# A five-stage hybrid transformer kernel: prologue order and buffers, paired block products in the delta attention, and the mixture's norm and stores moved into its body

## The chip, the cores and the metric

The kernel runs on one core of one Trainium2 chip. The metric is the device time of one execution in microseconds. The engines are TensorE (PE), VectorE (DVE), ScalarE (ACT), GpSimd (POOL) and SyncE (SP), which issues nearly all DMAs. All data are float32, and a float32 matmul shows in the trace as two matmul instructions (a transpose as one).

## What is computed

x has 4 sequences of 1024 tokens with 128 features. Four residual layers follow each other, each on a layer-normed x:

```python
x = x + delta_attention(layernorm(x))   # 8 heads; q, k, v by short convs (4 taps) and silu; beta, decay g
x = x + mixture(layernorm(x))           # 15 experts, top 3 of a softmax, and one shared expert
x = x + decay_attention(layernorm(x))   # 2 heads of 64, state decays by 1 - w
x = x + mixture(layernorm(x))
# delta attention, per token, head and each of 3 inner steps:
S = S * exp(g); S = S + b_i * k_i (v_i - k_i S); o = q S
# then o is rms-normed, gated with silu(x Wg) and projected by Wo
```

## The kernel before

**Prologue** (`prologue`, L124). Tokens lie as rows in four blocks. For each block TensorE turns the raw rows (`raw`) and the normed rows (`hat`) into feature columns, ScalarE keeps them (`keep_x` L248, `keep_xn` L259) and squares the centred rows (`square` L253), VectorE centres and norms, GpSimd takes the power -1/2. Then come the gates, a softplus chain on VectorE, and per head a table of decays: VectorE builds `gm` (L369, two buffers), TensorE sums it (L243), ScalarE exponentiates (L284), VectorE masks (L377), and SP stores it in four DMAs, 32 in all (L191). The loop's loads of the table wait for these stores.

**Delta attention** (`delta_attention`, L382) is a hand-scheduled software pipeline of 128 steps (8 heads by 16 spans of 64 tokens of all 4 sequences; U = 8 units of 32 tokens). A step runs through three stages in one loop over f: stage f projects, convolves and multiplies keys and queries into Gram products; stage c = f - 11 does values, gate and the inversion's block products; stage r = f - 12 runs the recurrence, in two halves cc. Every engine has its own written order (SP L640, GpSimd L731, ScalarE L865, VectorE L1020, TensorE L1238) and waits for the others through semaphores. An engine executes in order, so a wait holds up all behind it. The names that matter:

- `k_tile`, `v_tile`, `gate_tile` (L1122): projections into two PSUM banks PP; `tap0` (ScalarE L788) and `tap1` to `tap3` (VectorE L953) are the conv; `vsilu`, `ksilu`, `qsilu`, `gate_` the silu on ScalarE.
- `ktr`, `vtr` (L1173, L1195): transposes into TG; `ksum_`, `kr` read TG on ScalarE, `vr` (L993) on VectorE; `gram` (L1185), then `ap` (L982) on VectorE; `ss_`, `rinv_`, `step_`, `es_` small scales on VectorE, `rk_` on GpSimd.
- The results go through DRAM: `kqg_store`, `rec_store`, `ap_store` write, `rec_load`, `da_load`, `y_load`, `dec_load` read. Every fourth step (a group) `at_load` brings a 32-wide triangular system, `subst` solves it on GpSimd in 12 spots per step, `x_store` stores X, and `xt` (ScalarE L863) turns it.
- `zm` (L1204), `wm` (L1213), `m3` (L1221) join the inverted blocks: per unit a 64x64 product of `apkB` and `Dd` into the single bank ZW, then `zev` (L844, L845), `w12`, `yev` on ScalarE.
- The recurrence, per half: `ks` (L1076), `rhs_` (DVE L901), `w_` (L1086), `wev` (ACT L778), `sr` (L1096), `sup` (DVE L912, needs `sg` of GpSimd), and `o_` (L1111, L1112), `mo_`, `fo_`, `osb_`, `ot`, `og_`, `out`, `acc_` for the output.

```python
for u in range(U):                                   # zm, L1203
    last = mm(ZW[0:64, u, :], apkB[N % 2][:, u, :], Dd[N % 2][:, u, :], start=True, stop=True)
```

**Mixture** (`normed_mixture`, L1269, run as f1 and f2). First all 8 tiles of 512 tokens are normed in column layout: `centre` and `variance` by matmuls, square root on ScalarE, reciprocal on VectorE, `replicate`, `norm`. Router logits go over `r_lt` (L1364), `r_tr` (L1370), `r_sub` (L1491), `r_exp`, `r_top`, `r_ct` (L1376), `r_cwt` (L1524); SP stores the weights and loads them broadcast over the partitions (gates). Then for each tile and each of 16 experts: `hidden` (L1387), relu (L1470), scaling by the gate (L1558), second product (L1418). The router of tile n + 1 is placed in the body of tile n.

**Decay attention** (`decay_attention`) norms its tiles in row layout (L1663, L1873 to L1890, L1672); its near products (L1720) are 64x64 blocks on all four quarters of the array, the two row halves into two PSUM banks. **Store** (`store_rows`, L84): turns x back, four 512 KB DMAs on SP. Between stages stands a barrier of all engines.

## Time and profile before

| | us |
|---|---|
| median of 3 runs (lowest, highest) | 3255.2 (3253.8, 3260.7) |
| the profiled execution: time | 3252.4 |
| its span, first to last instruction | 3250.6 |
| prologue | 0 to 80 |
| delta attention | 80 to 2475 |
| mixture f1 | 2477 to 2764 |
| decay attention | 2765 to 2953 |
| mixture f2 | 2955 to 3239 |
| store | 3240 to 3250.6 |

PE is busy 94% of the span, DVE 78%, ACT 70%, GpSimd 60%. A row of a timeline has the start, the duration, the engine, the line of the kernel, output and inputs, the number of instructions merged, and in brackets the idle time before it with what ended it. A matmul's end is modelled and its duration overlaps the next one, so the distance of two starts tells what it held of the queue.

### The profile page before, as it was taken

The numbers are of one execution on the slowest core, as the hardware profiler recorded it, in microseconds if no ns is written. First come the engines' busy times: TensorE is split into PE (matmuls) and PEld (weight loads), VectorE is DVE, ScalarE is ACT, GpSimd is POOL, SyncE is SP. The second block draws the span as 40 slices with busy tenths as digits, with TensorE's granted clock in tenths as the row PEclk, the third lists the DMA queues.
The fourth block names the chain that finished last, engine by engine and source line by source line (L and its number), as shares of the span: only waits on it lengthen the run. The fifth ranks groups of instructions, "written<-read, shape, count | busy, mean of one in ns | idle before, by whom it ended". The sixth has DMA issues, their size and how long they took to land. (4 is left out here: it accounts for less than half of the span.)

```text
span 3250.6 us, 83664 instructions
## 1 busy us (share of the span) xinstructions
PE 3046.8 (94%) x27404; PEld 2373.9 (73%) x27404; DVE 2528.6 (78%) x5801; ACT 2265.4 (70%) x6879; POOL 1956.2 (60%) x3107
## 2 busy tenths in 40 slices
PE   5669999999999999999999999999998999768998
PEld 3458888888888888888888888888775444455444
DVE  5669999999999999999999999999654444684443
ACT  4678888888888888888888888888543333323333
POOL 1588888888888888888888888888720000100000
PEclk8779999999999999999999999999998999869999
DMA  4356776767677676767767677766532232002323
GB/s 100 113 153 172 186 183 174 181 173 182 168 190 179 176 181 169 182 174 188 182 170 183 171 175 178 190 180 165 141 95 83 107 145 98 10 2 76 147 98 124
DMA packets 587912, 482.88 MB, mean 149 GB/s; under 512 B 464492, under 2 KB 504076, under 8 KB 581340
## 3 DMA queue, kind: packets, MB, share of 16 engines
q1 hardware_dynamic: 587484, 477.53, 55.5%
q8 instruction: 225, 3.69, 0.5%
q14 instruction: 203, 1.66, 0.2%
HBM read 285.52 MB, written 191.86 MB: 147 GB/s over the span
## 5 line engine op out<-in xcount | busy, mean ns | idle before, releaser
L953 DVE SCALAR_TENSOR_TENSOR conv_k<-PP,tk,conv_k 128x256 f32<-128x256 f32 x1536 | 723.4, 479 | 62.9 <-ACT conv_k L788 35.1
L726 POOL TENSOR_TENSOR X<-X,tmp 96x31 f32<-96x31 f32 (+15 forms) x992 | 534.1, 538 | 77.7
L953 DVE SCALAR_TENSOR_TENSOR conv_v<-PP,tv,conv_v 128x256 f32<-128x256 f32 x1152 | 539.4, 477 | 45.1 <-ACT conv_v L788 35.5
L723 POOL TENSOR_TENSOR tmp<-At,X 96x31 f32<-96x31 f32 (+15 forms) x992 | 486.1, 490 | 63.0 <-DMA At<-n_d 4.8
L1122 PE MATMUL PP<-xn,wk 128*128 128x268 f32 x1024 | 344.6, 421 | 33.7 <-DVE conv_k L953 25.1
L709 POOL TENSOR_TENSOR rk<-ss,half 96x8 f32<-96x8 f32 x128 | 209.5, 1637 | 175.3 <-DVE ss L921 175.3
L691 POOL TENSOR_TENSOR Sg<-S,gend 128x512 f32<-128x512 f32 x256 | 266.1, 1039 | 59.3 <-DVE S L912 59.3
L760 ACT ACTIVATE recA<-TG,es 96x128 f32<-96x128 f32 x1024 | 284.9, 368 | 8.7 <-DVE es L946 8.7
L788 ACT ACTIVATE conv_k<-PP,tk 128x256 f32<-128x256 f32 x512 | 245.1, 480 | 60.1 <-PE PP L1122 53.4
L752 ACT ACTIVATE recA<-TG 128x128 f32<-128x128 f32 x1024 | 265.5, 272 | 25.3 <-PE TG L1173 25.3
L1086 PE MATMUL RB<-rhs,Yf 96*96 96x128 f32 x2048 | 269.1, 274 | 14.6 <-DVE rhs L901 14.3
L778 ACT ACTIVATE ws<-RB 96x512 f32<-96x512 f32 x256 | 151.6, 592 | 183.0 <-PE RB L1086 180.2
L1076 PE MATMUL RA<-S,kqgB 128*96 128x128 f32 x2048 | 276.2, 278 | 1.0 <-DVE S L912 1.0
L1096 PE MATMUL RA<-ws,recB 96*128 96x128 f32 x2048 | 271.1, 275 | 0.2 <-ACT ws L778 0.2
L1086 PEld LDWEIGHTS RB<-rhs,Yf 96*96 96x96 f32 x2048 | 242.2, 163 | 37.0 <-DVE rhs L901 24.6
L1096 PEld LDWEIGHTS RA<-ws,recB 96*128 96x128 f32 x2048 | 259.2, 192 | 8.0 <-ACT ws L778 0.8
L1185 PE MATMUL TG<-kq 128*96 128x128 f32 x1888 | 245.3, 273 | 1.2 <-ACT recA L760 1.0
L1076 PEld LDWEIGHTS RA<-S,kqgB 128*96 128x96 f32 x2048 | 233.4, 163 | 13.0 <-DVE S L912 4.4
L676 POOL TENSOR_TENSOR kqgA<-kq,gdec 128x768 f32<-128x768 f32 x128 | 203.2, 1588 | 39.3 <-ACT kq L829 32.6
L1122 PE MATMUL PP<-xn,wv 128*128 128x268 f32 x768 | 218.5, 391 | 2.3 <-DVE conv_k L953 2.3
L1185 PEld LDWEIGHTS TG<-kq 128*96 128x96 f32 x1888 | 219.0, 163 | 2.2 <-ACT recA L760 2.2
L1122 PEld LDWEIGHTS PP<-xn,wk 128*128 128x128 f32 x1024 | 163.8, 200 | 64.5 <-issue 34.5
(280 smaller groups left out, 6787.9 us busy)
## 6 DMA issues: line engine op xcount, KB each, us to landing
kqg_d<-kqgA SPq DMA_DIRECT2D x128, 512.0 KB, 6.2
kqgB<-kqg_d SPq DMA_DIRECT2D x128, 512.0 KB, 4.3
rec_d<-recA SPq DMA_DIRECT2D x128, 480.0 KB, 3.4
recB<-rec_d SPq DMA_DIRECT2D x128, 480.0 KB, 5.8
f1gates<-f1gates_d SPq DMA_DIRECT2D x24, 1024.0 KB, 6.7
f2gates<-f2gates_d SPq DMA_DIRECT2D x24, 1024.0 KB, 6.7
gdec<-gdec_d SPq DMA_DIRECT2D x128, 128.0 KB, 5.6
apk_d<-apkA SPq DMA_DIRECT2D x128, 128.0 KB, 3.3
```

What stands on the lines that cost most here:

```text
L691: nc.gpsimd.tensor_tensor(Sg[:, :, :], S[cc][:, :, :], d.broadcast_to([128, B, 128]), ALU.mult).then_inc(sg_ev[cc], 1)
L723: nc.gpsimd.tensor_tensor(t, At[q % 2][:, j, j + 1:].unsqueeze(2).broadcast_to(sh), X[q % 2][:, j, 0:cols].unsqueeze(1).broadcast_to(sh), ...
L726: nc.gpsimd.tensor_tensor(x, x, t, ALU.subtract).then_inc(sub_ev, 1)
L752: last = nc.scalar.activation(recA[N % 2][:, u * 128:(u + 1) * 128], TG[:, u, :], ACT.Square, accum_out=ksum[:, u:u + 1])
L760: last = nc.scalar.activation(recA[N % 2][0:R, u * 128:(u + 1) * 128], TG[0:R, u, :], ACT.Copy, scale=es[:, u, TC - 1:TC])
L788: nc.scalar.activation(acc, src[:, :, 0:SPAN], ACT.Copy, scale=w).then_inc(tap0_ev[i], 1)
L953: return nc.vector.scalar_tensor_tensor(acc, src[:, :, j:j + SPAN], w[:, j:j + 1], acc, ALU.mult, ALU.add)
L1076: last = mm(RA[0:R, b, :], kqgB[N % 2][:, b * NCC + cc, 0:R], S[cc][:, b, :], start=True, stop=True)
L1086: last = mm(RB[0:R, b, :], Yf[N % 2][:, b * NCC + cc, :], rhs[:, b, :], start=True, stop=True)
L1096: last = mm(RA[:, b, :], recB[N % 2][:, u * 128:(u + 1) * 128], ws[cc][:, b, :], start=True, stop=True)
L1122: mm(out, w, x, start=True, stop=True).then_inc(tile_mm[i], 1)
L1185: last = mm(gram_bank(N, hf)[0:R, u % HU, :], kq[N % 2][:, u, 0:R], kq[N % 2][:, u, :], start=True, stop=True)
```

## The change

The prologue's four engine orders change, `gm` gets four buffers, and the last of the four table stores of each head is issued by ScalarE. In the delta attention `apkB` and `Dd` hold their two halves of units on two partition halves, `zm` alternates between them, and their loads are split; `zev` reads the two halves; and all five written orders change. The mixture norms a tile in row layout inside the body, two tiles ahead, with three PSUM banks for `hidden` in place of four; logits come directly in row layout, with the bias added on VectorE (`r_sub`). In f2 each tile is turned back and stored by ScalarE one tile later, and the call of `store_rows` goes.

```diff
--- before.py
+++ after.py
...
-        gm = sb("gm", [128, 2, NC, TC])
+        DEEP = 4
+        gm = sb("gm", [128, DEEP, NC, TC])
...
+        def keep_table(eng, h, b):
+            eng.dma_start(g.edec_d[h, :, :, b, :], ex[TC * b:TC * (b + 1), h, :].rearrange("t (s x) -> t s x", x=SPAN)).then_inc(g.edec_out[h], 16)
...
             for h in range(NH):
                 sp.wait_ge(mask_ev, h + 1)
-                for b in range(B):
-                    sp.dma_start(g.edec_d[h, :, :, b, :], ex[TC * b:TC * (b + 1), h, :].rearrange("t (s x) -> t s x", x=SPAN)).then_inc(g.edec_out[h], 16)
+                for b in range(B - 1):
+                    keep_table(sp, h, b)
...
             raw(0)
             raw(1)
+            raw(2)
             hat(0)
-            raw(2)
+            raw(3)
             pe.wait_ge(w_in, 16 * 7)
             hat(1)
             gates(0)
-            raw(3)
             hat(2)
             gates(1)
+            gates(2)
             hat(3)
-            gates(2)
             gates(3)
...
+                square(q)
                 keep_x(q)
-                square(q)
-                if q:
-                    keep_xn(q - 1)
+                if q >= 2:
+                    keep_xn(q - 2)
+            keep_xn(B - 2)
             keep_xn(B - 1)
...
             for h in range(NH):
                 act.wait_ge(ge_mm, h + 1)
                 nc.scalar.activation(ex[:, h, :], GE[h % 2][:, :, :].rearrange("p a x -> p (a x)"), ACT.Exp).then_inc(ex_ev, 1)
+                if h:
+                    act.wait_ge(mask_ev, h)
+                    keep_table(nc.scalar, h - 1, B - 1)
+            act.wait_ge(mask_ev, NH)
+            keep_table(nc.scalar, NH - 1, B - 1)
...
                 total(q)
                 mean(q)
+                centre(q)
                 var_eps(q - 1)
-                centre(q)
-                norm(q - 1)
+                if q >= 2:
+                    norm(q - 2)
+            norm(B - 2)
             var_eps(B - 1)
             norm(B - 1)
...
-                need(dve, ge_mm, h - 2)
-                nc.vector.tensor_tensor(gm[:, h % 2, :, :], gt[:, h, :].unsqueeze(2).broadcast_to([128, NC, TC]), upto, ALU.mult).then_inc(gm_ev, 1)
+                need(dve, ge_mm, h - DEEP)
+                nc.vector.tensor_tensor(gm[:, h % DEEP, :, :], gt[:, h, :].unsqueeze(2).broadcast_to([128, NC, TC]), upto, ALU.mult).then_inc(gm_ev, 1)
             dve.wait_ge(gt_ev, 1)
-            sums(0)
-            sums(1)
+            for h in range(DEEP - 1):
+                sums(h)
...
                 nc.vector.tensor_tensor(x, x, upto, ALU.mult).then_inc(mask_ev, 1)
-                if h + 2 < NH:
-                    sums(h + 2)
+                if h + DEEP - 1 < NH:
+                    sums(h + DEEP - 1)
...
-        apkB, Dd = two("apkB", [64, U, 64]), two("Dd", [64, U, 64])
+        apkB, Dd = two("apkB", [128, HU, 64]), two("Dd", [128, HU, 64])
...
-                sp.dma_start(apkB[N % 2][:, :, :], apk_d[slot(N)]).then_inc(ld_da[N % 2], 16)
+                for hf in range(2):
+                    sp.dma_start(apkB[N % 2][64 * hf:64 * hf + 64, :, :], half(apk_d[slot(N)], hf)).then_inc(ld_da[N % 2], 16)
                 sp.wait_ge(st_x[q % 2], uses(q))
                 for b in range(2):
                     o = slice(BLK * b, BLK * (b + 1))
-                    sp.dma_start(Dd[N % 2][o, :, o], x_d[q, lanes(N, b)].rearrange("u r c -> r u c")).then_inc(ld_da[N % 2], 16)
+                    for hf in range(2):
+                        rows = slice(64 * hf + BLK * b, 64 * hf + BLK * b + BLK)
+                        sp.dma_start(Dd[N % 2][rows, :, o], x_d[q, lanes(N, b)][hf * HU:(hf + 1) * HU].rearrange("u r c -> r u c")).then_inc(ld_da[N % 2], 16)
...
+                rec_load(c)
                 at_load(*group_at(f, GROUP + 1))
                 x_store(*group_at(f, 2 * GROUP + 1))
-                rec_load(c)
+                dec_load(f)
                 da_load(c + 1)
                 weights(*divmod(f, KSTEPS))
-                dec_load(f)
-                kqg_store(f - 1)
+                y_load(c + 1)
                 rec_store(f - 1)
                 ap_store(f - 1)
-                y_load(c + 1)
+                kqg_store(f - 1)
...
+                fo_(r - 1)
+                sg(r, 0)
+                subst(*group_at(f - 1, GROUP + 1), range(10, 12))
+                kqg(f - 1)
+                rk_(f - 1)
+                sg(r, 1)
+                subst(*group_at(f, GROUP + 1), range(0, 9))
                 x_zero(*group_at(f, 3))
-                fo_(r - 1)
-                kqg(f - 1)
-                sg(r, 0)
-                rk_(f - 1)
-                subst(*group_at(f, GROUP + 1), range(0, 6))
-                sg(r, 1)
-                subst(*group_at(f, GROUP + 1), range(6, 12))
+                subst(*group_at(f, GROUP + 1), range(9, 10))
...
+                for hf in range(2):
+                    nc.scalar.activation(half(Zt, hf)[32:64, :, 0:32], ZW[64 * hf:64 * hf + 32, 0:HU, 0:32], ACT.Copy, scale=-1.0)
+                    last = nc.scalar.activation(half(Zt, hf)[64:96, :, :], ZW[64 * hf + 32:64 * hf + 64, 0:HU, :], ACT.Copy, scale=-1.0)
+                last.then_inc(zev_ev, 1)
...
-                xt(*group_at(f, 2 * GROUP + 1))
                 tap0(c, "v0")
+                mo_(r - 1, 1)
+                ksum_(f - 1, 1)
                 tap0(c, "v1")
-                ksum_(f - 1, 1)
                 ksum_(f - 1, 0)
                 wev(r, 0)
                 tap0(c, "v2")
+                xt(*group_at(f, 2 * GROUP + 1))
                 gate_(c)
                 zev(c)
                 tap0(f, "k1")
                 mo_(r, 0)
                 tap0(f, "k0")
+                kr(f - 1, 1)
                 kr(f - 1, 0)
+                w12(c)
+                q2_(f - 1)
+                tap0(f, "k2")
+                tap0(f, "q")
                 vsilu(c)
-                kr(f - 1, 1)
-                tap0(f, "k2")
-                w12(c)
                 wev(r, 1)
-                q2_(f - 1)
-                tap0(f, "q")
-                mo_(r, 1)
                 yev(c)
                 ksilu(f)
                 qsilu(f)
...
                 tap1(c, "v0")
+                tap2(c, "v0")
+                vr(c - 1, 0)
+                tap3(c, "v0")
                 osb_(r - 1)
-                tap2(c, "v0")
                 rhs_(r, 0)
-                tap3(c, "v0")
                 tap1(c, "v1")
...
                 acc_(r - 1)
+                step_(f - 1)
                 tap1(c, "v2")
-                step_(f - 1)
                 tap2(c, "v2")
                 tap3(c, "v2")
+                es_(f - 1)
                 sup(r, 0)
-                es_(f - 1)
                 tap1(f, "k1")
+                tap2(f, "k1")
                 tap1(f, "k0")
                 tap2(f, "k0")
                 tap3(f, "k0")
+                tap3(f, "k1")
                 rhs_(r, 1)
-                tap2(f, "k1")
-                ap(f - 1, 0)
-                tap3(f, "k1")
+                ap(f - 1, 1)
                 tap1(f, "k2")
                 tap2(f, "k2")
-                ap(f - 1, 1)
                 tap3(f, "k2")
                 tap1(f, "q")
                 tap2(f, "q")
                 tap3(f, "q")
                 vr(c, 1)
+                ap(f - 1, 0)
                 sup(r, 1)
-                vr(c, 0)
...
+                pe.wait_ge(ld_da[N % 2], 6 * uses(N))
...
-                for u in range(U):
-                    last = mm(ZW[0:64, u, :], apkB[N % 2][:, u, :], Dd[N % 2][:, u, :], start=True, stop=True)
+                for u in range(HU):
+                    for hf in range(2):
+                        o = slice(64 * hf, 64 * hf + 64)
+                        last = mm(ZW[o, u, :], apkB[N % 2][o, u, :], Dd[N % 2][o, u, :], start=True, stop=True)
...
                 v_tile(c, 0)
+                o_(r - 1, 1)
+                ktr(f - 1, 1)
+                vtr(c - 1, 0)
                 v_tile(c, 1)
-                ktr(f - 1, 1)
                 ks(r, 0)
                 ktr(f - 1, 0)
                 zm(c)
...
                 ks(r, 1)
+                gram(f - 1, 1)
+                k_tile(f, 2)
+                k_tile(f, 3)
+                m3(c)
+                w_(r, 1)
                 gram(f - 1, 0)
-                k_tile(f, 2)
-                w_(r, 1)
-                gram(f - 1, 1)
-                k_tile(f, 3)
-                o_(r, 1)
-                m3(c)
                 vtr(c, 1)
-                vtr(c, 0)
                 sr(r, 1)
...
+def normed_mixture(nc, g, tag, last=False):
...
+        rows = sb("rows", [128, 2, 4, 128])
...
+        WIDE = 3
+        ph = [pb(f"ph{i}") for i in range(WIDE)]
...
+        pl, pt, pr = pb("pl"), pb("pt"), pb("pr")
+        turn_bank = lambda n: (py[1] if n == 1 else pr)[:, :].rearrange("p (a d) -> p a d", a=4)
...
-            def centre(i):
-            def variance(i):
-            def replicate(i):
-            def r_lt(n):
...
+            def rows_of(n):
...
+                for a in range(4):
+                    end = nc.tensor.transpose(turn_bank(n)[:, a, :], x_of(n)[:, a * 128:(a + 1) * 128], g.ident[:, :])
+                end.then_inc(rows_mm, 1)
+            def hat(n):
...
+                pe.wait_ge(hat_ev, n + 1)
+                for a in range(4):
+                    end = nc.tensor.transpose(turn_bank(n)[:, a, :], rows[:, n % 2, a, :], g.ident[:, :])
+                end.then_inc(hat_mm, 1)
+            def r_lg(n):
...
-            def r_tr(n):
...
+                pe.wait_ge(xn_ev, n + 1)
...
                 for a in range(4):
-                    last = mm(pt[:, a * NE:(a + 1) * NE], lt[:, a * 128:(a + 1) * 128], g.ident[0:NE, 0:NE], start=True, stop=True)
...
+                    end = mm(pt[:, a * NE:a * NE + E_N], xn_of(n)[:, a * 128:(a + 1) * 128], rw[:, :], start=True, stop=True)
+                end.then_inc(lg_mm, 1)
+            def store_turn(n):
+                pe.wait_ge(acc_ev, n + 1)
+                pe.wait_ge(xn_ev, min(n + 3, NT))
...
+                for a in range(4):
+                    end = nc.tensor.transpose(turn_bank(0)[:, a, :], x_of(n)[:, a * 128:(a + 1) * 128], g.ident[:, :])
+                end.then_inc(st_mm, 1)
...
+                if e == 0:
+                    pe.wait_ge(xn_ev, n + 1)
+                if e >= WIDE:
+                    pe.wait_ge(relu[e - WIDE], n + 1)
...
-                mm(ph[e % DEEP][:, :], w1[:, e, :], xn_of(n), start=True, stop=True).then_inc(h_mm[e], 1)
...
+                mm(ph[(n * NE + e) % WIDE][:, :], w1[:, e, :], xn_of(n), start=True, stop=True).then_inc(h_mm[e], 1)
+            rows_of(0)
+            rows_of(1)
+            hat(0)
+            r_lg(0)
+            hat(1)
...
+            r_ct(0)
...
+                    if e == 1:
+                        rows_of(n + 2)
+                    if e == 11:
+                        hat(n + 2)
                     if n + 1 < NT:
                         if e == 0:
-                            r_lt(n + 1)
-                        if e == 2:
-                            r_tr(n + 1)
+                            r_lg(n + 1)
                         if e == 7:
                             r_ct(n + 1)
+                    if last and n and e == 14:
+                        store_turn(n - 1)
+            if last:
+                store_turn(NT - 1)
...
+            def square(n):
...
+                act.wait_ge(cent_ev, n + 1)
...
+                for a in range(4):
+                    end = nc.scalar.activation(sq[:, a, :], rows[:, n % 2, a, :], ACT.Square, accum_out=var[:, n % 2, a:a + 1])
+                end.then_inc(sq_ev, 1)
+            def keep_xn(n):
...
+                act.wait_ge(hat_mm, n + 1)
+                nc.scalar.activation(xn_of(n).rearrange("p (a d) -> p a d", a=4), turn_bank(n), ACT.Copy).then_inc(xn_ev, 1)
+            def keep_out(n):
+                act.wait_ge(st_mm, n + 1)
...
+                nc.scalar.activation(xo[:, n % 2, :, :], turn_bank(0), ACT.Copy).then_inc(st_ev, 1)
...
+                dst = d["out"].rearrange("b t d -> (b t) d")[TILE * n:TILE * (n + 1), :].rearrange("(a p) d -> p a d", p=128)
+                nc.scalar.dma_start(dst, xo[:, n % 2, :, :]).then_inc(stored[n % 2], 16)
...
+            square(0)
+            square(1)
+            keep_xn(0)
+            keep_xn(1)
+            r_exp(0)
...
+                        if e == 3:
                             r_exp(n + 1)
+                    if e == 6:
+                        square(n + 2)
+                    if e == 13:
+                        keep_xn(n + 2)
+                    if last and n and e == 15:
+                        keep_out(n - 1)
+            if last:
+                keep_out(NT - 1)
...
+                nc.gpsimd.tensor_tensor(rs[:, n % 2, :], var[:, n % 2, :], mhalf[:, :], ALU.pow).then_inc(rs_ev, 1)
...
+                nc.vector.tensor_reduce(nm[:, n % 2, :], turn_bank(n), AX.X, ALU.add).then_inc(sum_ev, 1)
...
+                nc.vector.tensor_tensor(rows[:, n % 2, :, :], turn_bank(n), spread(nm, n), ALU.add).then_inc(cent_ev, 1)
...
+                nc.vector.tensor_tensor(rows[:, n % 2, :, :], rows[:, n % 2, :, :], spread(rs, n), ALU.mult).then_inc(hat_ev, 1)
...
+            centre(0)
+            centre(1)
+            var_eps(0)
+            norm(0)
+            var_eps(1)
+            norm(1)
+            r_sub(0)
+            r_top(0)
...
+                    if e == 4:
+                        centre(n + 2)
+                    if e == 7:
+                        var_eps(n + 2)
+                    if e == 10:
+                        norm(n + 2)
                     if n + 1 < NT:
-                        if e == 3:
+                        if e == 2:
                             r_sub(n + 1)
                         if e == 5:
                             r_top(n + 1)
...
-        normed_mixture(nc, g, "f2")
-        store_rows(nc, g)
+        normed_mixture(nc, g, "f2", last=True)
...
```

## Rows read from the trace of the kernel before

**Rows 1.** Stretch by stretch: length, busy (instructions) of PE, PEld, DVE, ACT, POOL; PEclk; DMA share; GB/s.

```profile
240.00:2300.00 2060.00, 2052.49 (x20942) 1783.37 (x20941) 1894.54 (x4417) 1767.95 (x5727) 1751.48 (x2792) 1.00 0.71 178
```

**Rows 2.** Timeline of TensorE: zm in three successive steps.

```profile
1228.81 1.14 PE L1204 MATMUL ZW<-Dd,apkB 64*64 64x64 f32 x16
...
1246.33 1.14 PE L1204 MATMUL ZW<-Dd,apkB 64*64 64x64 f32 x16
...
1264.61 1.14 PE L1204 MATMUL ZW<-Dd,apkB 64*64 64x64 f32 x16
```

**Rows 3.** Waits from 240 to 2300 us: total us, times, longest.

```profile
ACT ws L778 <- PE RB L1086: 123.0, 117, 1.2
```

**Rows 4.** Timeline of TensorE: what follows zm, and near products.

```profile
1265.69 0.44 PE L1229 MATMUL SD<-ident,osb 128*128 128x128 f32 x2
...
2793.58 1.16 PE L1720 MATMUL b_pair<-b_rF,b_kB 64*64 64x64 f32 x64
```

**Rows 5.** Timeline of ScalarE in one step: wev, gate_, zev.

```profile
1213.71 0.59 ACT L778 ACTIVATE ws<-RB 96x512 f32<-96x512 f32 x1 [1.17 <-PE RB L1086]
...
1215.03 0.38 ACT L810 ACTIVATE gate<-PP 128x256 f32<-128x256 f32 x1 [0.37 <-PE PP L1122]
1215.44 0.37 ACT L844 ACTIVATE Zt<-ZW 32x256 f32<-32x256 f32 x1
1215.82 0.59 ACT L845 ACTIVATE Zt<-ZW 32x512 f32<-32x512 f32 x1
```

**Rows 6.** Groups by form, ScalarE: busy us, mean ns, idle us before.

```profile
L863 ACT ACTIVATE At<-X 96x1024 f32<-96x1024 f32 x32 | 64.5, 2015 | 3.9 <-POOL X L726 3.9
```

**Rows 7.** Timelines of SP and VectorE: the last stage of the prologue.

```profile
56.86 22.38 SPq L191 DMA_DIRECT2D edec_d<-ex  x32
...
74.35 1.23 DVE L377 TENSOR_TENSOR ex<-ex,p_upto 128x1024 f32<-128x1024 f32 x1 [1.04 <-ACT ex L284]
```

**Rows 8.** Waits of SP's queue from 240 to 2300 us.

```profile
SPq L121 <- ACT recA L760: 450.2, 116, 5.7
```

**Rows 9.** Timeline of TensorE in the drain: w_ and two zm.

```profile
2393.37 1.11 PE L1086 MATMUL RB<-rhs,Yf 96*96 96x128 f32 x8 [0.78 <-DVE rhs L901]
...
2400.03 1.14 PE L1204 MATMUL ZW<-Dd,apkB 64*64 64x64 f32 x16
...
2415.16 1.14 PE L1204 MATMUL ZW<-Dd,apkB 64*64 64x64 f32 x16
```

**Rows 10.** Timelines of TensorE and VectorE: heads of both mixtures and the decay attention.

```profile
2477.01 3.75 PE L1343 MATMUL f1ph<-xT,centre 128*128 128x512 f32 x4 [2.13 <-PEq L78]
...
2508.04 0.67 DVE L1524 COPY f1cwt<-f1pl 16x512 f32<-16x512 f32 x1
...
2515.76 1.91 PE L1418 MATMUL f1py<-f1hs,f1w 128*128 128x512 f32 x2
...
2524.35 0.22 DVE L1491 TENSOR_REDUCE f1mx<-f1pt 128x4 f32<-128x60 f32 x1 [2.15 <-PE f1pt L1370]
...
2528.78 0.22 DVE L1517 SCALAR_TENSOR_TENSOR f1cw<-f1m,f1p 128x60 f32<-128x60 f32 x1
...
2765.42 0.91 PE L1663 MATMUL b_pair<-ident,xT 128*128 128x128 f32 x4 [2.12 <-PEq L78]
...
2774.89 2.07 PE L1680 MATMUL b_pair<-xn,b_w 128*128 128x512 f32 x2
...
2954.99 1.95 PE L1343 MATMUL f2ph<-xT,centre 128*128 128x512 f32 x4 [1.73 <-PEq L78]
...
2991.36 2.07 PE L1418 MATMUL f2py<-f2hs,f2w 128*128 128x512 f32 x2 [1.45 <-DVE f2hs L1558]
```

**Rows 11.** Timeline of TensorE: r_lt and r_tr within a tile.

```profile
2707.69 1.03 PE L1364 MATMUL f1pl<-xn,f1rw 128*16 128x512 f32 x2
...
2712.29 1.06 PE L1370 MATMUL f1pt<-ident,f1lt 16*128 16x16 f32 x8
```

**Rows 12.** Timeline of VectorE: the last add of f2.

```profile
3238.49 0.69 DVE L1543 TENSOR_TENSOR xT<-f2py,xT 128x512 f32<-128x512 f32 x1 [1.43 <-PE f2py L1418]
```

More of the change, by code:

```diff
@@ L1375, in r_ct @@
                 for a in range(4):
-                    last = nc.tensor.transpose(pl[0:NE, a * 128:(a + 1) * 128], cw[:, a, :], g.ident[:, :])
-                last.then_inc(ct_mm, 1)
+                    end = nc.tensor.transpose(pl[0:NE, a * 128:(a + 1) * 128], cw[:, a, :], g.ident[:, :])
+                end.then_inc(ct_mm, 1)
             def hidden(n, e):
@@ L1469, in _ @@
                         need(act, hs_ev[NE + e - DEEP], n - 1)
[L1470 removed]
+                    nc.scalar.activation(hr[:, e % DEEP, :], ph[(n * NE + e) % WIDE][:, :], ACT.Relu, bias=b1[:, e:e + 1]).then_inc(relu[e], 1)
                     if n + 1 < NT:
[L1472 to L1474 removed]
+                        if e == 3:
@@ L1477, in _ @@
         @block.vector
         def _(dve):
[L1479 to L1490 removed]
+            spread = lambda t, n: t[:, n % 2, :].unsqueeze(2).broadcast_to([128, 4, 128])
@@ L1504, in r_top @@
                 for a in range(4):
-                    last = nc.vector.max(top[:, a, :], p20[:, a, :])
-                last.then_inc(top_ev, 1)
+                    end = nc.vector.max(top[:, a, :], p20[:, a, :])
+                end.then_inc(top_ev, 1)
                 dve.wait_ge(top_ev, n + 1)
@@ L1512, in r_top @@
                 for a in range(4):
-                    last = nc.vector.match_replace(m20[:, a, :], top[:, a, :], p20[:, a, :], -2.0)
-                last.then_inc(m_ev, 1)
+                    end = nc.vector.match_replace(m20[:, a, :], top[:, a, :], p20[:, a, :], -2.0)
+                end.then_inc(m_ev, 1)
                 dve.wait_ge(m_ev, n + 1)
```

207 lines of the change are left out of this document (66 added, 141 removed).

## The prediction

> **What bounds the kernel now.** I read the busy time by stage first, then the TensorE timeline of the delta loop, then the waits, then the two ends of every stage. The delta loop takes 2.2 of 3.25 ms. In its steady part TensorE is busy 99.6% of the time at a granted clock of 1.00 (2.4 GHz), VectorE 92%, ScalarE 86%, GpSimd 85% [rows 1]. 20942 matmul records at 180 a step, or 4417 VectorE records at 38 a step, give 116.3 steps in 2060 us: 17.71 us a step. The block product zm starts 17.52 us after its predecessor in three steps of four and 18.28 us in the fourth, where ScalarE turns the finished inverse (xt) [rows 2]. So TensorE's own queue is the bound in three steps of four, and 0.76 us of ScalarE in the fourth. ScalarE's free time sits in front of wev: 123 us in 117 steps, 1.05 a step [rows 3].
>
> **The profiled execution** took 3252.4 us (span 3250.6); the median of the three runs shown is 3255.2. Sums go against 3252.4; 2.8 us are added at the end.
>
> **zm in pairs.** Today its 16 instructions hold the queue from 1264.61 to 1265.69, 1.08 us. The near products of the other attention have the same shape (64x64 weights, 64 columns), lie on all four quarters of the array, and put 64 instructions in 1.16 us where zm puts 16 in 1.14 [rows 2, 4]. So disjoint quarters run beside each other; two at once make zm 0.54 us. Bounds: 0.3 if short instructions gain more, 1.1 if the pair does not overlap. I take 0.54: a TensorE step of 17.52 - 0.54 = 16.98 us.
> That row writes its two row halves to two PSUM banks, though; the new zm writes both to the single bank ZW, at different partitions. The Trainium skill, page TensorEngine Tiling (Array Packing), section Restrictions and Gotchas, says that different row tiles cannot access the same PSUM bank simultaneously. By that rule zm stays at 1.08 us and the step's gain is nothing; no row here decides it.
>
> **What else the step needs.** zev reads two halves, four activations in place of two: today 0.37 + 0.59 us [rows 5], in halves about 0.27 + 0.38 twice, 0.3 more (between 0, if cost goes by columns, and 1.0, if it goes by instruction). Busy per step at 17.71 us: ScalarE 15.2, now 15.5; VectorE 16.3; GpSimd 15.1 [rows 1]. All stay under 16.98, VectorE by only 0.7. The reordering mostly preserves instruction counts and gives rhs_(r,1) two matmul groups more cover. It brings wev(r,1), yev, ksilu, qsilu and the next ktr close behind each other: after w_(r,1) TensorE has only gram, vtr, sr, v0 and o_ before ktr needs qsilu. Laying out trace durations in the new order, I find 0.1 to 0.3 us of slack at ktr and as much on VectorE. I allow 0.05 us a step for stalls (0 to 0.5).
> xt (2.0 us [rows 6]) moves from the head of ScalarE's order, where the wev wait of 1.17 us behind it swallowed most of it, to just behind wev(r,0) and before gate_, where 0.37 us are idle [rows 5]. Queued behind it are gate_, zev (wm waits), tap0 k1 (VectorE waits), kr, w12 and wev(r,1). Up to 1.6 us may reach TensorE; slack before wm and m3 returns some. I take 1.1 in every fourth step (0.3 to 1.6).
> Mean step 16.98 + 0.05 + 1.1/4 = 17.3, against 17.71: 0.4 x 117 = **47 us** (ends: 85 and 0).
> SP gets three more DMAs a step (apkB in 2, Dd in 4). One costs 0.70 us of its queue (32 in 22.38 us [rows 7]): 2.1 us, against 450/116 = 3.9 us a step in which SP waits for ScalarE's kr alone [rows 8]. y_load moves ahead of the three stores and waits for w_(r,1); behind it stand rec_store, ap_store, kqg_store and the next loads, none needed before the next step. rec_load, first in the order, waits for o_(r-1,1), second on TensorE. x_store waits for xt, with dec_load and da_load behind: 2 us later, under a step ahead of use. On GpSimd sg and kqg come forward, two small substitution spots fall a step later, still ahead of xt. Nothing for all these; the cover is the idle time just named. The Trainium skill, page DMA: Bandwidth & Descriptors, section Rules for kernel authors, advises against splitting a transfer by partition halves, since the halves share the same engines. By that rule the split gains nothing in transfer and costs SP's issues, which the last sum prices.
>
> **Filling and draining.** The 12 filling steps wait on conv and silu chains; the change is neutral there (+-3 us). In the drain a step is 15.13 us (2400.03 to 2415.16), with w_(r,1) waiting 0.78 us for rhs [rows 9]. m3 now covers that wait, o_ and half of vtr leave the stretch between w_ and sr, zm loses 0.54: about 1.2 us for each of 11 steps, **13 us** (5 to 17).
>
> **Prologue.** SP's 32 stores of the decay table take 22.4 us and end at 79.2, the last thing before the loop; the masks end at 75.6, after waits such as 1.04 us for ex [rows 7]. With 24 stores on SP (16.8 us from 56.9) and four gm buffers, masks end near 71.5 and stores near 73.7: 5.5 us. Earlier squares and gates in another order: 2.5 (0 to 7). Together **8 us** (4 to 12).
>
> **Mixture.** The first w2 product starts 38.75 us after the first matmul in f1 (2477.01 to 2515.76) and 36.4 in f2 (2954.99 to 2991.36) [rows 10], since all eight tiles are normed first. The new head has this chain: rows, centre, square, pow, norm, turn as in the decay attention, whose first product follows the first transpose by 9.5 us [rows 10]; logits 1.1 [rows 11]; softmax and top three, 4.65 from the maximum to cw, plus 0.2 for the bias [rows 10]; turn 0.9 (four transposes at half clock, as at 2765.42); and 7.7 us from the copy of cwt through the gates' DMA to the product [rows 10]. Sum 24.1: 14.6 saved in f1, 12.3 in f2. In a tile, r_lt (1.0 us [rows 11]) goes from seven tiles, rows_of and hat (four transposes each, half of that 0.91 at full clock) come in six; the small logit products take r_tr's place: 1.2 saved. f2's seven store turns add 3.5. VectorE gets 1.6 us of centring before the 2.1 us of top three, against 1.8 us between a scaled tile and its product: just hidden. Keep_out and its DMA issue stand on ScalarE behind the last relu and hold up the next tile's first one; that product stands behind b2 and two others, which hides it. WIDE = 3 costs nothing: hidden(e+2) follows the product that needed relu(e-1) anyway. Mixtures: **16 + 10 us** (20 to 32 together).
>
> **Tail.** The last add starts at 3238.49 [rows 12] and the span ends at 3250.6. A barrier, 32 transposes and four 512 KB stores become 4 transposes, one copy, one issue and 256 KB: **5 us** (3 to 6).
>
> Sum 47 + 13 + 8 + 26 + 5 = 99: 3252.4 - 99 = 3153, with the offset 3156.
>
> **Rivals.**
> A pair that does not overlap (one PSUM bank): zm 1.08, steps at 17.5 to 17.7, the drain saves half. For it: no row has two row halves in one bank. Against: the outputs share no partition. 3255 - (5 + 7 + 8 + 26 + 5) = 3204. Chance 0.12.
> ScalarE or VectorE takes over: VectorE is 0.7 us under the new TensorE step, and stalls of 0.3 give 17.5 to 17.6, saving 18: 3185. Chance 0.2.
> xt hidden and no stalls: 17.0 a step, 85 us: 3116. Chance 0.08.
> Slower: SP becomes the bound. It has 19 issues a step, 22 where a group changes, in one queue with waits for ap, w_ and xt. At 0.70 each that is 13 to 15 us. The outside gains of 52 us are used up at 0.44 us a step, 18.15 us; that needs 0.96 us an issue. Then zm waits for Dd. At 1.0 an issue, 19 us a step: 3255 - 52 + 151 = 3354. For it: SP is the most changed queue. Against: 3.9 us of wait. Chance 0.05.
> My forecast, 3130 to 3180: 0.55.
>
> **How the numbers follow.** A measurement of this kernel tells about 0.2%, 6.5 us, from no change. Every case but the slower one lies 50 us or more under 3255: faster 0.94, same 0.02, slower 0.04. The range 3108 to 3205 takes in the three faster rivals with the bounds of the step, and leaves out the slower one and half of the smallest.
>
> **What would show it.** zm's 16 instructions in 0.5 to 0.6 us; starts of zm 17.0 apart and about 18.1 in the fourth; drain steps near 14; first loop matmul near 73; first w2 products 24 us behind the first transposes; tiles of f1 at 31.4. It is wrong if the steps stay at 17.5 with zm short (another engine leads), if zm stays at 1.08, or if TensorE waits at L1204 for Dd.

## The result and the profile after

The changed kernel took **3322.6 us** (median of 4 runs, 3317.0 to 3325.6) against 3257.9 for the kernel before on the same chip: ratio 1.0198, interval 1.0178 to 1.0217. It is 2% slower, where 3156 was forecast. The profiled execution spans 3323.8 us, 73.2 more than before (3250.6).

The first reading is by stage: the table of stretches of the changed kernel, cut where its first loop matmul, f1 and f2 start (length, busy time and instructions of PE, PEld, DVE, ACT, POOL, granted clock, DMA share, GB/s).

```profile
0.00:71.90 71.90, 38.84 (x356) 26.18 (x357) 42.05 (x53) 33.00 (x97) 8.82 (x13) 0.88 0.52 113
71.90:240.00 168.10, 100.61 (x528) 80.87 (x529) 110.37 (x265) 113.11 (x430) 113.84 (x171) 0.75 0.47 128
240.00:2400.00 2160.00, 2050.44 (x20823) 1726.44 (x20822) 1961.71 (x4394) 1767.68 (x5928) 1739.36 (x2778) 0.99 0.63 169
2400.00:2585.10 185.10, 161.21 (x1693) 132.89 (x1691) 103.40 (x208) 84.38 (x205) 75.86 (x131) 0.95 0.36 96
2585.10:3045.90 460.80, 397.83 (x3096) 224.97 (x3097) 271.01 (x579) 157.81 (x334) 23.59 (x27) 0.87 0.20 76
3045.90:3323.80 277.90, 262.26 (x720) 122.03 (x720) 132.02 (x362) 108.17 (x217) 8.13 (x9) 0.94 0.34 130
```

| part | before, us | after, us | difference | forecast |
|---|---|---|---|---|
| prologue, to the first loop matmul | 80.6 | 71.9 | -8.7 | -8 |
| delta attention, to f1 | 2396.4 | 2513.2 | +116.8 | -60 |
| f1 and decay attention | 478.0 | 460.8 | -17.2 | -16 |
| f2 and store | 295.6 | 277.9 | -17.7 | -15 |

Everything outside the loop came as forecast. The whole miss lies in the delta attention. Its rhythm is read from the starts of zm on the timeline of TensorE, as in [rows 2]:

```profile
1202.03 0.68 PE L1190 MATMUL ZW<-Dd,apkB 64*64 64x64 f32 x16
1219.88 0.68 PE L1190 MATMUL ZW<-Dd,apkB 64*64 64x64 f32 x16
1238.53 0.68 PE L1190 MATMUL ZW<-Dd,apkB 64*64 64x64 f32 x16
1258.37 0.68 PE L1190 MATMUL ZW<-Dd,apkB 64*64 64x64 f32 x16
1276.33 0.68 PE L1190 MATMUL ZW<-Dd,apkB 64*64 64x64 f32 x16
```

zm itself did what was hoped: 0.68 us in place of 1.14, so the pairs overlap. The steps are 17.85, 18.65, 19.84 and 17.96 us, mean 18.57, against 17.71 before. Over 108 steps of the steady loop the mean is 18.67: the third of these steps is the uneven one, 19.1 to 23.2 us, 20.4 in the mean. Three things stand out, each on its own engine.

**VectorE: ss.** The group of this one small instruction over 240 to 2400 us (busy, mean ns of one):

```profile
L905 DVE TENSOR_SCALAR ss<-ksum 128x8 f32<-128x8 f32 x115 | 121.1, 1053 | 0.0
```

Before it took 162 ns (18.8 us for 116), so its 8 elements per partition are no work for a microsecond. The timelines of VectorE and GpSimd in one step say what it stands beside:

```profile
1242.17 1.83 DVE L905 TENSOR_SCALAR ss<-ksum 128x8 f32<-128x8 f32 x1
...
1241.70 1.58 POOL L657 TENSOR_TENSOR kqgA<-kq,gdec 128x768 f32<-128x768 f32 x1
1243.24 0.73 POOL L658 TENSOR_TENSOR kqgA<-kq,gdec 128x256 f32<-128x256 f32 x1
1243.92 0.19 POOL L660 COPY gend<-gdec 128x8 f32<-128x8 f32 x1
1244.08 1.64 POOL L690 TENSOR_TENSOR rk<-ss,half 96x8 f32<-96x8 f32 x1
```

ss ends at 1244.00, 0.03 us after the second of GpSimd's two kqg products (1243.97). In the steady loop before, GpSimd stood idle at this point, waiting for ss with rk_. The new order put kqg into that place. How it reaches TensorE shows in another step (VectorE, VectorE, TensorE):

```profile
1204.43 1.08 DVE L905 TENSOR_SCALAR ss<-ksum 128x8 f32<-128x8 f32 x1
...
1206.03 1.51 DVE L937 SCALAR_TENSOR_TENSOR conv_v<-PP,tv,conv_v 128x256 f32<-128x256 f32 x3
...
1207.64 0.69 PE L1106 MATMUL PP<-xn,wk 128*128 128x268 f32 x2 [0.42 <-issue]
```

The last conv_v ends at 1207.54, and only then does the k product go on. The profile puts this one wait to issue; over the stretch it puts such waits to conv_v (PEld is TensorE's weight load):

```profile
PEld PP L1106 <- DVE conv_v L937: 52.0, 71, 1.1
```

**GpSimd: At.** Waits over 240 to 2400 us (total us, times, longest):

```profile
ACT ws L760 <- PE RB L1070: 134.6, 116, 4.7
...
POOL tmp L704 <- DMA At<-n_d: 93.5, 29, 4.8
...
DVE osb L984 <- POOL fo L683: 56.4, 29, 3.5
...
PEld SD L1215 <- DVE osb L984: 40.0, 29, 2.9
```

Before, the waits for At were 4.2 us in all. 29 is the number of groups in this stretch, so this is one step in four. Of the first row, wev's wait in front of ScalarE, 123 us stood before too [rows 3]. SP's timeline has the load behind two large ones:

```profile
1221.09 0.36 SPq L568 DMA_DIRECT2D kqgB<-kqg_d  x1
1221.50 0.79 SPq L570 DMA_DIRECT2D recB<-rec_d  x1
1222.40 0.43 SPq L605 DMA_DIRECT2D At<-n_d  x1
```

From issue to landing At takes 3.8 us in the median before and 6.8 now, and its issue itself stands 1.3 us behind that of kqgB. The chain down to TensorE, row by row (GpSimd, GpSimd, VectorE, TensorE):

```profile
1229.55 0.23 POOL L704 TENSOR_TENSOR tmp<-At,X 96x31 f32<-96x31 f32 x1 [2.80 <-DMA At<-n_d]
...
1238.54 0.19 POOL L681 TENSOR_TENSOR fo<-mo,q 128x2 f32<-128x2 f32 x1
...
1239.55 0.42 DVE L984 TENSOR_TENSOR osb<-SD,fo 128x256 f32<-128x256 f32 x1 [1.51 <-POOL fo L683]
...
1240.03 0.44 PE L1215 MATMUL SD<-ident,osb 128*128 128x128 f32 x2 [0.81 <-DVE osb L984]
```

The new order has nine spots of the substitution between sg(r,1) and the next fo_, so 2.8 us at their head arrive at the output's scale, and from there in both queues behind it. Over the 29 groups the step is 19.1 us after the shortest of these waits (2.1) and 22.3 and 23.2 after the two longest (4.8 and 4.4).

**ScalarE: xt.** ScalarE, then the TensorE product that gate_ holds up:

```profile
1222.70 1.99 ACT L847 ACTIVATE At<-X 96x1024 f32<-96x1024 f32 x1
1224.59 0.37 ACT L792 ACTIVATE gate<-PP 128x256 f32<-128x256 f32 x1
...
1225.01 0.72 PE L1106 MATMUL PP<-xn,wk 128*128 128x268 f32 x2 [0.99 <-ACT gate L792]
```

This is the 18.65 us step.

### The profile page after: what moved, and what is told of

It reads as the page before. It is cut to its first block and busy times, and to the rows that moved or that the text cites. A ratio compares the mean times of both kernels' runs of the same rounds, so it can differ in the third digit from the quotient of the medians.

```text
span 3323.8 us, 84081 instructions
## 1 busy us (share of the span) xinstructions
PE 3011.2 (91%) x27212; PEld 2313.4 (70%) x27212; DVE 2620.6 (79%) x5859; ACT 2264.2 (68%) x7209; POOL 1969.6 (59%) x3125
## 5 line engine op out<-in xcount | busy, mean ns | idle before, releaser
L937 DVE SCALAR_TENSOR_TENSOR conv_k<-PP,tk,conv_k 128x256 f32<-128x256 f32 x1536 | 707.5, 481 | 117.7 <-ACT conv_k L770 85.2
L937 DVE SCALAR_TENSOR_TENSOR conv_v<-PP,tv,conv_v 128x256 f32<-128x256 f32 x1152 | 549.7, 477 | 21.8 <-ACT conv_v L770 3.5
L1106 PE MATMUL PP<-xn,wk 128*128 128x268 f32 x1024 | 324.3, 421 | 115.8 <-DVE conv_k L937 40.2
L1070 PE MATMUL RB<-rhs,Yf 96*96 96x128 f32 x2048 | 283.3, 282 | 7.3 <-DVE rhs L885 5.6
L1106 PEld LDWEIGHTS PP<-xn,wk 128*128 128x128 f32 x1024 | 171.8, 197 | 167.7 <-DVE conv_v L937 53.3
L770 ACT ACTIVATE conv_k<-PP,tk 128x256 f32<-128x256 f32 x512 | 229.8, 474 | 82.2 <-PE PP L1106 75.0
L742 ACT ACTIVATE recA<-TG,es 96x128 f32<-96x128 f32 x1024 | 274.0, 371 | 7.8 <-DVE es L930 7.8
L1060 PEld LDWEIGHTS RA<-S,kqgB 128*96 128x96 f32 x2048 | 240.8, 163 | 22.9 <-DVE S L896 0.9
L1106 PE MATMUL PP<-xn,wv 128*128 128x268 f32 x768 | 242.7, 397 | 0.0
L657 POOL TENSOR_TENSOR kqgA<-kq,gdec 128x768 f32<-128x768 f32 x128 | 202.7, 1584 | 33.8 <-ACT kq L811 20.5
```

Source lines behind the costliest of these rows:

```text
L742: last = nc.scalar.activation(recA[N % 2][0:R, u * 128:(u + 1) * 128], TG[0:R, u, :], ACT.Copy, scale=es[:, u, TC - 1:TC])
L770: nc.scalar.activation(acc, src[:, :, 0:SPAN], ACT.Copy, scale=w).then_inc(tap0_ev[i], 1)
L937: return nc.vector.scalar_tensor_tensor(acc, src[:, :, j:j + SPAN], w[:, j:j + 1], acc, ALU.mult, ALU.add)
L1060: last = mm(RA[0:R, b, :], kqgB[N % 2][:, b * NCC + cc, 0:R], S[cc][:, b, :], start=True, stop=True)
L1070: last = mm(RB[0:R, b, :], Yf[N % 2][:, b * NCC + cc, :], rhs[:, b, :], start=True, stop=True)
L1106: mm(out, w, x, start=True, stop=True).then_inc(tile_mm[i], 1)
```

## The experiments

Each kernel was timed beside the kernel before, whose medians were 3254.1 us in the first four experiments, 3260.3 in the next four (`at_first`, `ss_at`, `gp_at_xt`, `xt_split`) and 3258.7 in the last four. So ratios are compared; 0.001 is 3.3 us. Steps given as four numbers are distances of zm in a cycle of four, as above.

### The outside alone, and the pair in the old orders

`outside`: the changed kernel with `delta_attention` of before.

> The changed kernel with the whole delta attention of before; prologue, mixtures and stores as changed. By stage the two traces differ by -8.7 us (prologue), -17.2 (f1 and decay attention) and -17.7 (f2 and store). Theory A (the parts add, the loop alone costs): 3258 - 44 = 3214. Rival B (the new prologue or mixtures disturb the loop, for example through ScalarE's stores or the clock): 3230 or more.

Measured: 3211.6 us, ratio 0.9871 (0.9856 to 0.9885). The parts outside the loop are worth 42.5 us and don't disturb it.

`pair_old_orders`: the pairs, the six loads and the four zev, in the old order of all five engines.

> The changed kernel with the five written orders of before, but with zm in pairs, its six loads and the four zev. Theory A (the pair is a gain, the new orders are the whole loss): zm holds the queue 0.61 us in place of 1.07, steps near 17.1, 3214 - 54 = 3160. Rival B (the pair's three more DMAs on SP or the four zev make the step long): 3250 to 3320, with waits at zm or wm. Rival C (another engine leads at 17.5): 3200 to 3214.

Measured: 3197.0 us, ratio 0.9826 (0.9805 to 0.9848), 15 us below `outside`. The steps are 17.1, 17.1, 18.3 and 17.5: TensorE's two clean steps fell by 0.42, and the two that ScalarE's xt sets stayed. That is 0.21 a step, 25 us. The result lies between theory A and rival C, and each was right about two steps of the four; rival B is out, since TensorE waits for no load at zm and only 1.0 us in all for zev before the drain. Part of the 25 us was given back in the drain: four of its steps are 15.5 us, and after them zm starts 17.1 us apart (2371.47, 2388.53, 2405.59), and not 15.13 as in [rows 9]. Stretches of this kernel's drain, and the same view of the kernel before:

```profile
2330.00:2370.00 40.00, 34.38 (x371) 29.08 (x370) 19.29 (x39) 18.41 (x41) 10.49 (x21) 0.96 0.35 89
2370.00:2390.00 20.00, 17.71 (x179) 14.57 (x178) 11.73 (x25) 7.92 (x19) 4.02 (x5) 0.91 0.36 104
```

```profile
2400.00:2430.00 30.00, 26.94 (x296) 23.00 (x296) 17.33 (x36) 13.32 (x30) 5.69 (x9) 1.00 0.33 88
```

The granted clock, the last but two of the columns, is 0.91 and was 1.00; within a step vtr holds 1.74 us in place of 0.92, so the clock was at its 1.2 GHz level there. What TensorE did before is visible: it idled 0.21, 0.33, 0.78 and 0.68 us in each of these steps, and zm is shorter. The kernel before had the waits of 0.78 and 0.68 too, at 1.00; whether the rest is what took the clock down, no run shows.

### ss in a form of its own

```diff
-                nc.vector.tensor_scalar(ss[:, :], ksum[:, :], 1e-6, None, ALU.add)
+                nc.vector.tensor_reduce(ss[:, :], ksum[:, :].unsqueeze(2), AX.X, ALU.add)
```

> The changed kernel with ss formed by a tensor_reduce over an axis of one in place of a tensor_scalar; this leaves out the 1e-6 added to the sum of squares. Theory A (ss stands 1.05 us in place of 0.16 because VectorE can't start it while GpSimd's kqg runs, and VectorE sets the step): ss back at about 0.2 us, the 0.4 us gap of TensorE before the k product goes, 0.4 to 0.9 us a step, 3240 to 3276. Rival B (VectorE has room, the loss is at the fourth step alone): 3315 to 3323 though ss is short. Rival C (ss waits for something that has nothing to do with its form): ss stays at 1.05 us, 3323.

Measured: 3284.9 us, ratio 1.0101 (1.0080 to 1.0121), 0.0097 or 32 us under the changed kernel. The group over the same stretch:

```profile
L905 DVE TENSOR_REDUCE ss<-ksum 128x8 f32<-128x8 f32 x116 | 17.5, 151 | 0.0
```

In the same place of the same order, beside the same kqg, it takes 0.15 us. The clean steps go from 17.9 and 17.7 to 17.4 both, and the waits for conv_v shown above from 52.0 to 21.0 us. Rivals B and C are out: it was the form. Theory A was right in its mechanism, but the time is 9 us above the upper end of its range, since two steps of the four are set elsewhere: the one of 18.65 us didn't move, and the one behind the late At fell from 20.4 to 19.9 in the mean.

### GpSimd's old order alone

> The changed kernel with GpSimd's written order of before alone. Theory A (GpSimd's order costs twice: kqg on top of ss, and fo behind the substitution that waits for At): ss at 0.16 us, TensorE's wait of up to 2.9 us for osb gone, 3210 to 3240. Rival B (the late load of At, issued behind rec_load, costs in any order of GpSimd): ss short, but 1 to 2 us remain in the fourth step, 3250 to 3280. Rival C (xt's place on ScalarE is the main cost): 3300 or more.

Measured: 3384.6 us, ratio 1.0396 (1.0379 to 1.0412). A miss for all three: ss is back at 0.16 us in the median (0.30 in the mean), and the kernel is 0.0198 or 65 us slower than the changed one. By its number this is rival C, but the reason given there was xt, and the waits say At. GpSimd reaches its first spot earlier and waits longer for At, 5.7 us a time; the step goes to 22 to 23 us:

```profile
POOL tmp L704 <- DMA At<-n_d: 159.5, 28, 6.8
```

So the new GpSimd order was milder to the late load than the old one. What the load itself costs, the next run shows.

### at_load back in front

```diff
-                rec_load(c)
                 at_load(*group_at(f, GROUP + 1))
+                rec_load(c)
                 x_store(*group_at(f, 2 * GROUP + 1))
```

> The changed kernel with one line of SyncE's order put back: at_load stands before rec_load, so that the load of At isn't behind the 512 and 480 KB loads of kqgB and recB. Theory A (the fourth step's 20.2 us come from GpSimd waiting 3.2 us for At, then fo, osb and ot late): GpSimd's wait for At near 0, the fourth step near 17.9, 2.3 x 29 = 67 us less, 3256. Rival B (fo is late because nine spots of substitution stand before it, whenever At lands): 3310 to 3323.

Measured: 3243.9 us, ratio 0.9950 (0.9934 to 0.9967): one line put back takes 81 us off, and the kernel is then 0.5% faster than before. The uneven step, which the expectations call the fourth, is 17.7 us. Rival B is out, and theory A's 67 us were too few. Over the stretch shown before, the waits for At fell from 93.5 to 5.6 us, and from issue to landing it takes 3.7 us in the median again, not 6.8 (the table of issues: count, KB each, median us to landing):

```profile
At<-n_d SPq DMA_DIRECT2D x30, 384.0 KB, 3.7
```

`ss_at` has both repairs.

> The changed kernel with both: ss by tensor_reduce (the 1e-6 left out) and at_load before rec_load. If the two causes are separate the gains add: 3285 - 67 = 3218, steps 17.4, 17.4, 18.6, 17.4. If the late At hid behind the long ss or the other way round, less: 3230 to 3250.

Measured: 3209.8 us, ratio 0.9843 (0.9829 to 0.9858). 0.0355 under the changed kernel, against 0.0097 + 0.0248 = 0.0345 for the two alone: separate causes that add. Steps 17.4, 17.4, 17.4, 18.65: mean 17.71, exactly the 17.71 of before.

`at_late_old` is the opposite test: the old orders with the pair, and rec_load ahead of at_load and x_store.

> The old orders with zm in pairs (3197), and rec_load put ahead of at_load on SyncE, nothing else. Theory A (the load of At lands about 3 us later behind kqgB and recB, and GpSimd's first spots stand at once behind rk in this order too): GpSimd waits for At, 1 to 3 us in every fourth step reach TensorE, 3225 to 3285. Rival B (the old GpSimd order has the room): 3195 to 3205.

Measured: 3298.9 us, ratio 1.0112 (1.0086 to 1.0138), 0.0286 or 93 us above `pair_old_orders`, and 14 us above the upper end of theory A. The step after the load goes from 17.5 to between 18.9 and 23.4 us (mean 21.2), At's landing from 3.8 to 6.6. Its waits show the same chain:

```profile
DVE osb L983 <- POOL fo L683: 84.1, 29, 4.2
POOL tmp L704 <- DMA At<-n_d: 82.7, 30, 7.4
...
PE SD L1214 <- DVE osb L983: 55.0, 30, 3.3
```

The swap alone, put into the old orders, costs more than the whole change lost in the end (93 against 65 us).

### What the pair and the orders are worth

`ss_at_single`: as `ss_at`, but zm, zev and the loads of before.

> The changed orders with ss by tensor_reduce (the 1e-6 left out) and at_load first, but zm, zev and the loads of before (one unit at a time, three loads, two activations). Theory A (TensorE leads in this loop and the pair is worth what it holds less of the queue, 0.46 us a step): 3210 + 0.46 x 117 = 3264. Rival B (VectorE or ScalarE leads, the pair is worth little, as its 15 us in the old orders may say): 3215 to 3235.

Measured: 3259.5 us, ratio 1.0003 (0.9994 to 1.0012), 0.0160 or 52 us above `ss_at`; zm's 16 instructions have 1.14 us again. Theory A: the pair is worth its 0.45 us a step (52 / 117), and in all four steps, the one with xt too (19.1 against 18.65).

How the orders compare is read from TensorE's timeline of one clean step: for each kind of instruction the distance from start to next start, waits taken out (a table worked out from these rows; steps starting at 1228.81, 1209.33, 1205.17 and 1202.03).

```
us held in one step       before  pair_old_orders  ss_at  changed
zm                          1.07             0.62   0.62     0.61
v products                  1.38             1.37   1.47     1.47
w_                          1.76             1.74   1.83     1.83
o_, second product          0.57             0.58   0.71     0.77
ktr                         0.96             0.97   1.02     1.03
all others                 11.78            11.82  11.75    11.72
sum                        17.52            17.10  17.40    17.43
waits                          0                0      0     0.42
```

In the new order the same instructions hold TensorE 0.3 us longer without a wait. The rows that grew are those of groups that stood together and are now apart (the v products of v0 and v1), or that have another neighbour; that the neighbour is the reason is read from this table, and no run tests it. The pair's 0.45 less becomes 0.12.

### Where xt stands

`gp_at_xt`: GpSimd's old order, at_load first, xt at the head of ScalarE's order.

> The changed kernel with GpSimd's order of before, at_load first and xt at the head of ScalarE's order as before; TensorE's, VectorE's and the rest of ScalarE's order as changed. Theory A (ss, At and xt's place are the whole loss, the new TensorE order costs only 0.3 us a step more than the old): steps 17.4 in three and about 18.2 in the fourth, mean 17.6, 3206. Rival B (the new orders of VectorE and ScalarE stall with the old one of GpSimd, as its order alone did): 3240 or more.

Measured: 3233.1 us, ratio 0.9918 (0.9903 to 0.9933). This is between the two, and 0.0075 or 24 us above `ss_at`. Steps 17.4, 19.0, 17.4, and 17.4 to 18.6: with xt at the head its step is 1.6 us over the clean one, where the place that the change gave it costs 1.25. GpSimd's order differs as well, though: xt waits 0.3 us a time for its last spot, and the waits for At are 26.2 us again. So the head is no better in these orders, but what the place alone is worth isn't shown.

`xt_split`: the old orders with the pair, xt in two halves over the system's columns.

```diff
                 ksum_(f - 1, 0)
+                xt(*group_at(f, 2 * GROUP + 1), 0)
                 wev(r, 0)
                 tap0(c, "v2")
+                xt(*group_at(f, 2 * GROUP + 1), 1)
                 gate_(c)
```

> The old orders with zm in pairs (3197) and xt cut into two halves of 1.0 us, one before wev(r,0), where ScalarE waits about 1.1 us, one before gate_, where it waits 0.6. Theory A (in the two steps at 18.3 and 17.5 ScalarE's xt is the bound): both fall to 17.1 to 17.4, up to 1.5/4 x 117 = 44 us, 3155 to 3170. Rival B (something else holds these steps): 3190 to 3200.

Measured: **3179.4 us**, ratio 0.9752 (0.9737 to 0.9766), the fastest of all. Steps 17.1, 17.1, 17.6, and 17.1 to 19.0 in the fourth. Of the 44 us expected at most, 24 came: the step of 18.3 fell by 0.7, but the one of 17.5 didn't fall (17.65 in the mean), so theory A holds in full for one of its two steps. In 8 of 29 groups the other did fall, to between 17.1 and 17.2; what held it in the rest is told under the last run.

> The changed orders with ss by tensor_reduce (the 1e-6 left out), at_load first, and xt in two halves, one ahead of wev(r,0) and one ahead of gate_. Theory A (xt is what makes the one step of 18.65 us among steps of 17.4): that step falls by about 1.0, 29 x 1.0 = 30 us under 3210, 3180. Then the new orders with every stall taken out are no better than the old ones with the pair and the same xt (3179). Rival B (the halves wait for GpSimd's last spots in this order): 3195 to 3210.

Measured: 3190.7 us, ratio 0.9797 (0.9780 to 0.9813), steps 17.4, 17.4, 18.0, 17.4: the special step fell by 0.6, not 1.0, and the result lies between the two expectations. With ss, At and xt all repaired the new orders still lose 0.0045, 15 us, to the old ones.

> The old orders, zm in pairs, xt in halves (3179), and the store of y taken out of x_store and put behind da_load on SyncE. In the run before SyncE waited 2.7 us in each fourth step for the second half of xt, with rec_load behind it. Theory A (that wait makes the fourth step's 17.2 to 19.0): 17.1 to 17.3 there, 0.5 x 29 = 15 us, 3160 to 3167. Rival B (it is another wait): 3175 to 3180.

Measured: 3182.8 us, ratio 0.9763 (0.9747 to 0.9779), no gain. The fourth step is still 17.1 to 21 us, so theory A falls. What makes it uneven can be read from both traces: it is At again. GpSimd waits for it 20.5 us here over 240 to 2300 us and 20.6 in `xt_split`, against 4.9 in `pair_old_orders`. In the 13 groups of this kernel where GpSimd doesn't wait for At, the fourth step is 17.15 to 17.19 us; in the 16 where it waits, the step is the longer the longer the wait, 17.52 after one of 0.24 and 20.97 after one of 2.69. That last one, row by row (GpSimd, then four rows of TensorE), and its stretch of 5 us:

```profile
2056.37 0.23 POOL L709 TENSOR_TENSOR tmp<-At,X 96x31 f32<-96x31 f32 x1 [2.69 <-DMA At<-n_d]
...
2066.94 0.68 PE L1198 MATMUL ZW<-Dd,apkB 64*64 64x64 f32 x16
2069.06 0.44 PE L1223 MATMUL SD<-ident,osb 128*128 128x128 f32 x2 [1.44 <-DVE osb L992]
2070.04 2.02 PE L1078 MATMUL RB<-rhs,Yf 96*96 96x128 f32 x8 [0.54 <-DVE rhs L893]
...
2087.91 0.68 PE L1198 MATMUL ZW<-Dd,apkB 64*64 64x64 f32 x16
```

```profile
2070.00:2075.00 5.00, 4.96 (x23) 4.57 (x24) 3.61 (x11) 1.89 (x5) 4.62 (x7) 0.66 0.80 228
```

TensorE's waits of 1.44 and 0.54 us are half of what the step is longer. The rest is clock: after them the granted clock is 0.66 for 5 us, and w_'s eight products take 2.02 us against 1.04. So a late load costs more than TensorE waits for it. Why the load lands late in some groups and not in others stays open. The drain is at 17.0 us a step here, and in `xt_split` at 15.5 after two steps of 17. Their stretches, first this kernel, then `xt_split`:

```profile
2360.00:2390.00 30.00, 25.84 (x261) 21.68 (x260) 14.96 (x31) 13.04 (x32) 4.92 (x7) 0.90 0.29 74
```

```profile
2360.00:2390.00 30.00, 25.83 (x288) 21.36 (x280) 16.65 (x35) 13.04 (x32) 5.96 (x8) 1.00 0.34 89
```

Both are busy for the same 25.8 us of 30, at a granted clock of 0.90 and 1.00, and one gets 10% more instructions through. Part of the busy time at 0.90 is instructions that take longer, so equally busy doesn't mean equal work.

## Why the prediction was wrong

**The forecast.** 47 + 13 us of gain in the loop were forecast and 117 of loss measured. The price of the pair (0.54, measured 0.45), xt (1.1, measured 1.25), the prologue (8, 8.7) and both mixtures with the tail (31, 35; the first w2 product of f1 follows the first transposes by 24.2 us, of f2 by 23.8, where 24.1 was summed) were right. So were six of the drain's last seven steps, 14.1 to 14.7 us where near 14 was forecast. Two of its sums are off by little: the rival without stalls adds up to 3118 us (3255 - 85 - 52), not 3116, and seven times r_lt less twelve times four transposes is about 1.6 us, not 1.2.

**The step that failed first** is the paragraph on SP: "Nothing for all these; the cover is the idle time just named." It went through SP's moved steps and left one out, at_load, which rec_load had passed. The error was to ask whether SP has room (it has: it waits 457.6 + 181.1 us in 116 steps, 5.5 a step, on two engines) and not what stands in front of each transfer and who waits for its landing. In the trace before, At is issued at 1246.32, lands 3.8 us later, and GpSimd's first spot starts at 1251.80: 1.7 us of slack, by the median landing, for a load that was put behind 992 KB and came 3.0 us later from issue to landing. Price, by putting the one line back or into the old orders: 81 us in this kernel, 93 in those.

**The second** is "On GpSimd sg and kqg come forward [...] Nothing". kqg came to stand beside ss, and ss went from 0.16 to 1.05 us: 32 us. [Rows 1] put VectorE 0.7 us under the new step; the extra 0.89 used that up. In the steady loop before, GpSimd waited for ss at rk_ each time, so those rows held no price of ss beside GpSimd. The filling steps of the same trace did (VectorE, then GpSimd twice):

```profile
209.96 1.66 DVE L921 TENSOR_SCALAR ss<-ksum 128x8 f32<-128x8 f32 x1 [3.88 <-ACT recA L752]
...
209.34 1.57 POOL L676 TENSOR_TENSOR kqgA<-kq,gdec 128x768 f32<-128x768 f32 x1
210.87 0.72 POOL L677 TENSOR_TENSOR kqgA<-kq,gdec 128x256 f32<-128x256 f32 x1
```

There too ss ends 0.03 us after the second product, in a kernel without the change. The Trainium skill has the rule, on the page SBUF — State Buffer, section Who interferes with whom: a `tensor_scalar` can enter a mode that takes a port pair shared with GpSimd, and then whichever is second waits for the whole instruction, while a `tensor_reduce` never contends. The trace agrees, 1.05 and 0.15 us in the same place; here ss waited for two instructions of GpSimd in a row, not for one.

**The third** is a term that was missing: "The reordering mostly preserves instruction counts" led to 17.52 - 0.54 = 16.98. Counts aren't held time; the new TensorE order costs 0.3 us in each step. With it the step is 17.40 and, with xt in one of four, 17.71, so that even without the two mishaps the steady loop gains nothing: `ss_at` lies only 0.0028, 9 us, under `outside`, and their intervals touch. What gain there is comes from the drain, with steps of 14.1 to 14.9 in most of it; the steady steps have the same mean of 17.71 in both.

**The rivals.** The rival of the single PSUM bank fell. By the rule that the Trainium skill states on the page TensorEngine Tiling (Array Packing), section Restrictions and Gotchas, zm would have stayed at 1.08 us; it holds 0.61, and the measurement decides. The slower rival named SP and the right side, at 0.05 and 3354 us, but its mechanism, a queue with too many issues, didn't occur. The three more DMAs cost SP 1.5 us (1.10 + 2.01 against 0.48 + 1.08), not 2.1, and zm never waited for Dd. "VectorE takes over" did occur in the clean steps, for a reason not named: TensorE waited 0.42 us in such a step, and 17.9 became 17.4 us once ss was short.

## What to carry over

When a transfer changes place in a queue, write down for each load what is issued ahead of it, when it lands and who waits; spare time of the queue says nothing about a landing. When an engine's order changes, look at what now runs at the same time on the engine next to it, above all VectorE's small instructions beside GpSimd. Look for the price in every stage of the trace, the filling too. And price a new order of TensorE by start-to-start distances: the new order cost 0.30 us a step here, two thirds of what the faster product gave.

## What was not expected of the hardware

A VectorE `tensor_scalar` on 8 elements per partition took up to 1.83 us beside GpSimd's products, and a `tensor_reduce` on the same data 0.15.

64x64 products on two different row and column quarters of the array, written to different partitions of one PSUM bank, overlap: 16 in 0.68 us against 1.14.

The drain's granted clock differs between kernels whose TensorE is busy for the same share of it: 0.89 to 0.96 in two of them (`pair_old_orders`, `y_later`), 1.00 in a third (`xt_split`), worth 1.5 us in a step. What decides it stays open.
